# The last tile's rows are turned once more, as fp32 and as fp32r, and the scaled difference is added to the result

## The reference, cut to what matters

```python
def _L1_ffn_ref(x, W, b, Wq, Wk, A, Bm):
    result = jnp.einsum('bsi,oi->bso', x, W) + b
    q = jnp.einsum('bsi,ni->bsn', x, Wq).reshape(Bt, S, E, DK)
    k = jnp.einsum('bsi,ni->bsn', x, Wk).reshape(Bt, S, E, DK)
    scores = jnp.einsum('bsed,bsed->bse', q, k) / math.sqrt(DK)
    w = jax.nn.softmax(scores, axis=-1)
    h = jnp.einsum('bsi,eri->bser', x, A)
    combined = jnp.einsum('bse,bser,eor->bso', w, h, Bm) * SCALING
    return result + combined
x = _layernorm(x + _L1_ffn_ref(x, ...), axis=-1)
```

## Time and profile before

| what | us |
|---|---|
| three runs, median | 1427.98 |
| lowest and highest | 1427.68, 1428.55 |
| the profiled execution | 1428.5 |
| its span, first to last instruction | 1426.7 |
| TensorE matmuls busy | 1412.0 |
| VectorE busy | 1019.6 |
| ScalarE busy | 891.3 |
| GpSimd busy | 774.1 |

### The profile page before, as it was taken

How to read it: one execution, slowest core, us unless ns; L and a number is a source line. 1 busy time by engine, 2 the same in 40 slices (tenths; PEclk the granted TensorE clock), 3 DMA queues, 4 the chain that set the end, 5 groups by cost and what they waited for, 6 DMA issues and landing times.

```text
span 1426.7 us, 30207 instructions
## 1 busy us (share of the span) xinstructions
PE 1412.0 (99%) x8769; PEld 1251.7 (88%) x8769; DVE 1019.6 (71%) x2528; ACT 891.3 (62%) x2445; POOL 774.1 (54%) x827
## 2 busy tenths in 40 slices
PE   9999999999999999999999999999999999999998
PEld 8999999998787888889889889889889889889886
DVE  5999999998968875665665665565565565665866
ACT  5888888887555576555555555555556556556621
POOL 3555555555040367765765665665665665664521
PEclk9999999999999999999999999999999999999999
DMA  5533333322445201101001001001001001000201
GB/s 196 168 92 96 93 95 94 94 64 50 133 134 175 83 30 55 36 30 59 29 29 59 29 29 59 29 29 59 29 29 59 29 29 59 29 29 29 82 19 42
DMA packets 56155, 92.60 MB, mean 65 GB/s; under 512 B 6064, under 2 KB 27312, under 8 KB 56112
## 3 DMA queue, kind: packets, MB, share of 16 engines
q1 hardware_dynamic: 55968, 91.93, 21.5%
q10 hardware_dynamic: 144, 0.13, 0.0%
HBM read 81.82 MB, written 2.10 MB: 59 GB/s over the span
## 4 chain that ended last, share of the span: by engine, by line
PE 92%; DVE 3%; ACT 1%; DMA 1%; issue 1%; POOL 1%; SPq 0%; POOLq 0%; DVEq 0%; ACTq 0%
PE c_bv L101 7%; PE c_bv L102 7%; PE c_bv L103 7%; PE c_bx L101 4%; PE c_bx L103 4%; PE c_bx L102 4%; PE h_bo L928 4%; PE c_by L103 4%; PE c_by L102 4%; PE h_bt L914 4%; PE c_by L101 4%; PE c_bt L2230 3%; PE h_bo L1427 2%; PE a_acc L1427 2%; PE h_bs L101 2%; PE h_bs L103 2%
## 5 line engine op out<-in xcount | busy, mean ns | idle before, releaser
L604 POOL TENSOR_TENSOR h_pr<-h_pr,h_rinv 128x512 f32<-128x512 f32 x128 | 133.2, 1041 | 137.9 <-DVE h_rinv L752 135.6
L1758 POOL TENSOR_TENSOR c_qk<-g_y,c_qk 128x512 fp32r<-128x512 f32 x96 | 124.1, 1292 | 153.0 <-ACT c_qk L1870 146.2
L1609 POOL TENSOR_TENSOR b_sw_lo<-b_slots,b_sw_hi 128x512 fp32r<-128x512 f32 (+1 forms) x128 | 148.4, 1159 | 10.2
L1607 POOL CAST b_sw_hi<-b_slots 128x512 fp32r<-128x512 f32 (+1 forms) x128 | 72.8, 569 | 143.9 <-DMA b_slots<-in_w_qk 124.0
L102 PE MATMUL c_bv<-b_wv_lo,g_xT_hi 128*128 128x256 f32 x496 | 138.8, 280 | 0.0
L101 PE MATMUL c_bv<-b_wv_hi,g_xT_hi 128*128 128x256 f32 x496 | 138.7, 280 | 0.0
L103 PE MATMUL c_bv<-b_wv_hi,g_xT_lo 128*128 128x256 f32 x496 | 138.6, 279 | 0.0
L1979 DVE TENSOR_TENSOR c_bo<-c_bo,g_wo 128x128 f32<-128x128 f32 x128 | 38.4, 300 | 122.5 <-ACT g_wo L1845 116.1
L1870 ACT ACTIVATE c_qk<-g_y 128x512 fp32r<-128x512 f32 x96 | 60.7, 632 | 99.2 <-DVE g_y L2016 69.2
L657 ACT ACTIVATE h_pr<-h_bs,h_nmax 128x256 f32<-128x256 f32 x256 | 119.0, 478 | 2.5 <-DVE h_nmax L747 2.4
L1835 ACT ACTIVATE c_pr<-c_pr,c_rinv 128x128 f32<-128x128 f32 (+1 forms) x256 | 101.9, 448 | 9.0 <-DVE c_rinv L1969 9.0
(11 more groups left out here) (479 smaller groups left out, 5186.4 us busy)
## 6 DMA issues: line engine op xcount, KB each, us to landing
f_wi<-in_w_ffn SPq DMA_DIRECT2D x66, 256.0 KB, 2.7
b_slots<-in_w_qk SPq DMA_DIRECT2D x64, 256.0 KB, 3.0
a_w<-in_w_head SPq DMA_DIRECT2D x28, 352.0 KB, 2.9
h_part<-in_w_ffn SPq DMA_DIRECT2D x32, 264.0 KB, 2.7
b_raw_v<-in_w_v SPq DMA_DIRECT2D x16, 512.0 KB, 4.5
b_raw_o<-in_w_o SPq DMA_DIRECT2D x16, 512.0 KB, 4.7
h_o_mix<-h_o_hi SPq DMA_DIRECT2D x62, 128.0 KB, 2.2
b_ffn_w<-in_w_ffn SPq DMA_DIRECT2D x4, 576.0 KB, 5.5
```

Source lines behind the costliest of these rows:

```text
L604: pool.tensor_tensor(pr[b][:, :, :], pr[b][:, :, :], rinv[b][:, :][:, :, None].to_broadcast([P, 2, S]), ALU.mult)\
L1607: pool.tensor_copy(self.sw[0][:, a:b], self.slots[:, a:b]).then_inc(self.s_whi, 1)
L1609: pool.tensor_tensor(self.sw[1][:, a:b], self.slots[:, a:b], f32(self.sw[0][:, a:b]), ALU.subtract)\
L1758: pool.tensor_tensor(lo, src, f32(hi), ALU.subtract).then_inc(s_sumlo, 1)
```

## The change

It adds instructions on three engines behind the work of the last tile, and puts one store behind them.

- SBUF: `yo_r` lies at the address of `yo[1]` (`under` frees its place at once and `yo[1]` takes it) and is declared fp32r. `ident_r`, `turned` and `diff` are new tiles.
- GpSimd, behind the last power (`s_rs` at NT + 1): copies the identity to `ident_r`, fp32r.
- TensorE, behind `combined_last`: waits for that copy and for both halves of the last tile, turns columns 0 to 255 of `yo[1]` as fp32 into `bx`, turns the same bytes three times as fp32r into `bw`, and does two matmuls of 512 columns into `bq0` that nobody reads.
- VectorE: waits for the last transpose, copies `bx` to `turned`, subtracts it from `bw` into `diff`, and adds a million times `diff` to the second half of `yo[1]`.
- ScalarE: issues the store of the second half one count of `s_yo` later, behind that addition.

```diff
-        yo = [k.sb(f"yo{i}", [P, HID]) for i in range(2)]
+        yo = [k.sb("yo0", [P, HID])]
+        yo_r = k.under("yo_r", [P, HID], F32R)
+        yo.append(k.sb("yo1", [P, HID]))
...
+        ident_r, turned, diff = k.sb("ident_r", [P, P], F32R), k.sb("turned", [P, 2 * P]), k.sb("diff", [P, 2 * P])
...
             rounds(pool, round_)
+            pool.wait_ge(s_rs, NT + 1)
+            pool.tensor_copy(ident_r[:, :], ident[:, :]).then_inc(s_rs, 1)
...
-            act.wait_ge(s_yo, NT + 1)
+            act.wait_ge(s_yo, NT + 2)
             act.dma_start(out[NT - 1, :, halves[1]], yo[1][:, halves[1]]).then_inc(s_out[1], 16)
...
+                dve.wait_ge(s_tx, NT + 1)
+                dve.tensor_copy(turned[:, :], bx[:, 0:2 * P]).then_inc(s_end, 1)
+                after(s_end, NEND * t + 1)
+                dve.tensor_tensor(diff[:, :], bw[:, 0:2 * P], turned[:, :], ALU.subtract).then_inc(s_end, 1)
+                after(s_end, NEND * t + 2)
+                dve.scalar_tensor_tensor(out=yo[1][:, halves[1]], in0=diff[:, :], scalar=1e6,
+                                         in1=yo[1][:, halves[1]], op0=ALU.mult, op1=ALU.add).then_inc(s_yo, 1)
...
+            def turned_twice():
+
+                pe.wait_ge(s_rs, NT + 2)
+                pe.wait_ge(s_yo, NT + 1)
+                for c in range(2):
+                    pe.transpose(bx[:, c * P:(c + 1) * P], yo[1][:, c * P:(c + 1) * P], ident[:, :])
+                for i in range(3):
+                    for c in range(2):
+                        m = pe.transpose(bw[:, c * P:(c + 1) * P].bitcast(F32R), yo_r[:, c * P:(c + 1) * P],
+                                         ident_r[:, :])
+                m.then_inc(s_tx, 1)
+                for c in range(2):
+                    pe.matmul(bq0[:, 0:HID], whT[0][:, :], bm[0], start=True, stop=True, skip_group_check=True)
...
                     combined_last()
+                    turned_twice()
```

## The result

The changed kernel takes 1431.01 us in the median of 18 runs (1429.96 to 1433.92), the kernel before 1428.05 us (18 runs, 1427.08 to 1429.77). The two medians lie 2.96 us apart. The ratio of the runs is estimated at 1.0017, with a 95% interval of 1.0011 to 1.0024: 2.4 us more, between 1.6 and 3.4. The forecast was 1430.8, "within 0.2%" at 0.50 and "slower" at 0.48.

The account below looks back on a forecast made before the run. The prediction took the chain behind the last matmul, ending in ScalarE's store, to bound the kernel. Issue 3.84 us later less 1.0 of landing gave +2.8 us on the 1427.98 median: 1430.8 us, range 1429.4 to 1432.3.

Parts of the forecast that it names:

- What bounds the kernel: Behind the last matmul: a chain of short steps to ScalarE's store; delaying its issue delays the end as much.
- GpSimd's copy hidden: Behind GpSimd's last power: the identity copy ends before VectorE's second half; no cost, uncovered at most 0.4 us.
- TensorE's wait and code: Before the transposes: weight load starts 0.06 us behind the second output half, code already there; cost nothing.
- Eight transposes, 2.20 us: TensorE's new block at half clock: seven spacings of 0.22 us plus a lead of 0.66, 2.20 us.
- The two matmuls: TensorE, behind the transposes: they signal nobody and finish under VectorE's steps and the landing; zero, uncovered 1.6 us.
- VectorE's three operations, 1.55 us: Between transposes and ScalarE's store: copy 0.41, difference and multiply-add 0.42 each, two gaps of 0.15; 1.55 us.
- The landing, -1.0: ScalarE's last store: issued later, it misses the first half and the instruction packet, landing in 1.9 instead of 2.9 us.
- rival 1: Last store: landing stays long, +3.1 to +3.84 us; sign: instruction packet between 1427.5 and 1429 with stragglers; chance 0.20.
- Sum: End of the kernel: store issued 3.84 us later, landing 1.0 us shorter, together +2.84 us.
- rival 2: TensorE's transposes: clock still full, block 1.22 us, total +1.8 us, 1429.8; chance 0.22.
- Rival 3: TensorE's transposes: fp32r costs like plain fp32 at half clock, +4.4 us in total, 1432.4; chance 0.05.
- Rival 4: ScalarE's store doesn't wait for the addition; time 1428.0, or 1427 with a shorter landing; chance 0.03.

Follow-up runs that it names:

- before_wait: The kernel before plus one wait for GpSimd's `nm_end` and one unread matmul at the end of TensorE's stream; ratio 0.9995 against the kernel before.
- the two late kernels: cold_turn, and the changed kernel with its six fp32r transposes as fp32; last landings 3.6 and 3.0 us, one run each.
- cold_turn: The changed kernel with TensorE's block also waiting for the landing of the first half's store; one run, 12.7 us from last matmul to end.
- after_third: The changed kernel, unedited, measured and profiled a third time; ratio 1.0017 against the kernel before.
- sooner: The changed kernel with TensorE waiting for the first output half only and the identity copied ahead of GpSimd's last power; ratio 1.0014 against the kernel before.
- warm_fill: The changed kernel with fifteen unread matmuls of 512 columns between the last real matmul and TensorE's new waits; ratio 1.0010 against the kernel before.

## Why the prediction was right

The total was right, 1431.01 us against 1430.8 and inside the range, and so was the chain: from the second output half over TensorE and VectorE to ScalarE's store, less a part given back by the landing. The block was priced too high, though, and the landing was short for a reason that the prediction had only in part. Term by term:

- *What bounds the kernel*: right for the chain of the change, which lies behind the last matmul; whether anything ahead of it is later because of the change stays open (below).
- *GpSimd's copy hidden*: right for TensorE's start, but not free. It makes the two output halves 0.06 us longer (0.79 against 0.73).
- *TensorE's wait and code*: the load starts 0.11 us behind the second half, I had 0.06. The code was there, also 0.4 us sooner.
- *Eight transposes, 2.20 us*: the step that was mis-sized. It measured 0.94, 1.03 and 1.45 us in three profiles. I priced all eight as fp32 transposes at half clock; an fp32r transpose costs 0.15 us there and not 0.22, and the clock was full under the whole block in one profile of three and under its first part in another. With all in fp32 and the clock at half it would have been nearly right (2.01).
- *The two matmuls*: zero, right.
- *VectorE's three operations, 1.55 us*: 1.57 in every profile, the copy out of PSUM as long as the two-input operations.
- *The landing, -1.0*: -1.1 to -1.2. That a packet held one engine was right; before_wait and the two late kernels show it both ways. The reason for the gain was not: I had let the packet stay where it was, and it moved with TensorE's new wait, from 4.3 us behind the last matmul to 8.3 to 8.7. It came at 1428.3, inside the stretch that I had named as the sign of rival 1, and was harmless because it started 1.3 to 1.9 us behind the issue. At 1.0 us behind the issue it costs 1.9 us (cold_turn), and only 0.3 us part after_third from that, so here luck helped. The 1.9 us for an undisturbed landing came from a row that doesn't show one; it measured 1.7.
- *Sum*: ScalarE's issue later by 2.7 to 3.2 instead of 3.84, the end by 1.5 to 2.1 instead of 2.84.

So the profiles of the end give less than predicted and less than the runs' best value (+2.4, +1.7 and +2.4 us in three measurements), though their intervals (from +0.4 to +3.7) hold 1.5 to 2.1. What fills the rest, if there is a rest, stays open, and that the median met 1430.8 owes something to it: by the end alone it would have been 1429.5 to 1430.1.

Two candidates stand in the traces, and neither was tested. The first is in the changed kernel itself: in an execution at half clock whose second packet came as early as in the first profile (8.27 us behind the last matmul, with the issue at 7.21), the packet would start 1.06 us behind the issue. At 1.01 and 1.05 us behind it the landings are 3.6 us (cold_turn) and 3.3 us (sooner's first half). No profile of the changed kernel caught that.

The second is ahead of the change. The last matmul starts at 1418.4 to 1419.4 in the four profiles without the change and at 1418.3 to 1421.9 in the ten with it or a part of it. Laid side by side by VectorE's instructions, the profiles part in the first 40 us (against the first profile of the kernel before, 0 to 0.6 us later without the change and 0.3 to 1.3 later with it) and between 290 and 585 us, and from there to the last matmul keep their distance to 0.1 us. Sooner's last matmul is the latest; it falls back by 1.5 us between 290 and 380 us, and in that stretch its granted clock was at 0.50 for a while, under a busy TensorE, as it was in warm_fill, which falls back by 0.8 us there. Windows of sooner (stretch, length, TensorE busy, granted clock, DMA share, GB/s):

```profile
363.00:365.00 2.00, 2.00 (x6) 0.50 0.00 0
```

No run here shows whether the mean of this scatter is shifted by the change.

Of the rivals, rival 2 (full clock, a block of 1.22) is what the first profile showed, in one execution of several, with a block still cheaper than its 1.22. Rival 1's mechanism is real, but the changed kernel escapes it in all three profiles. The packets are TensorE's own, as argued against it; but the change gives TensorE a new end too, which the argument left out. Rival 3 is refuted: fp32r is the cheaper type. Rival 4 is refuted by the timeline: ScalarE issues 0.03 us behind the addition.

## What to carry to other kernels

Work appended behind the last result costs its latency chain, step by step, and most steps can be read from like rows to a tenth of a microsecond; what can't is a block on an array that has just gone idle, whose clock differs from execution to execution, and a type that no row shows. Before pricing a final store, look at the instruction packets beside it: if its landing is longer than that of an equal store, work that moves either may gain or lose over a microsecond. Where the end of an idle engine's stream fetches code into the last stores, a wait ahead of its last instruction moves the fetch. A wait that is added for another reason moves it too, perhaps into a store that was free of it (tile 6's in before_wait, the first half's in sooner).

## What the runs showed of the hardware that I had not expected

- One 16 KB packet of instructions makes a 128 KB store to memory land in 2.7 to 3.6 instead of 1.7 to 1.8 us, if it starts between 0.1 and 1.05 us behind the store's issue (ScalarE's in five profiles, SyncE's in sooner). At 1.3 us behind and later (eight profiles) it did nothing. In the records a single one of such a store's 16 semaphore increments is late by more than 0.5 us.
- The packets at the end of TensorE's stream don't follow the array: eight matmuls more, 1.8 us of work, left them within 0.2 us of their place, one wait moved them by 1.2 to 1.4 us, measured from the last real matmul.
- In seven profiles TensorE did nothing between the last real matmul and the fall of the clock; there the fall came 2.6 to 4.1 us behind the start of that matmul. In the first two of the changed kernel the clock was still full when the block began, 4.2 us behind it. One profile is no evidence of the clock in the next.
- In a row of six with their weight loads, a transpose of 128x128 takes its turn in 0.11 us (fp32) and 0.09 (fp32r) at 2.4 GHz, 0.21 and 0.15 at 1.2 GHz.
